# A sixteen-sequence layer kernel on one core: an own order of steps for each engine, the next sequence's front moved among the exponentials, maxima in halves, expert weights in eight pieces

## The chip, the cores and the metric

One core of a Trainium2 chip runs the whole program. Its engines are PE (TensorE, matrix products), ACT (ScalarE), DVE (VectorE), POOL (GpSimd) and SP (SyncE, which here only issues DMAs); each works through its own list of instructions, and they meet at semaphores. The metric is the device time of one execution in microseconds. The kernel before takes 1146.2 us, the median of three runs (1144.76 to 1148.17).

## The reference

Sixteen sequences of 256 tokens with 256 features pass four residual layers:

```python
x = x + x @ weight[subject].T + bias[subject]               # L0: one of 8 weights for each sequence
x = x + zX*lap_x(x) + zY*lap_y(x) + zR*x*(1 - x)            # L1: neighbours in both directions
# L2: 16 heads of 16 columns; q and own key, value from the side input, keys and values from x
q = (side + b_self) @ Wq + bq; k = (x + b_prev) @ Wk + bk; v = x @ Wv + bv
score_prev = q @ k.T / 4, masked beyond seq_len; score_self = (q * k_self).sum(-1) / 4
x = x + softmax([score_prev, score_self]) @ [v, v_self] @ Wo + bo
# L3: two shared dense layers s0, s1 and one of three chosen by the label (eo): relu(x @ wi) @ wo, F = 1024
w = softmax(relu([eo[0], s0[0], s1[0]] @ g1) @ g2)
x = x + eo * w[0] + s0 * w[1] + s1 * w[2]
```

All of it is float32. The kernel splits operands into a high and a low part and adds three products (hi·hi, lo·hi, hi·lo) for each.

## The kernel before, in words

Tiles are 128 partitions by 512 columns: both halves of the features side by side. A sequence goes through three groups of steps. The **front** makes x1, q, ks, lap, vs, kp, vp (x after L0, query, own key, the neighbours of L1, own value, key, value) and "self", the own scores. q and k are cut in three 16-bit parts each and copied by SP's DMAs (`place`, L386, six for each) into q_rows and k_rows, where one head's scores are a single product. The **attention** runs S0 to S15 (scores of a head, of which DVE takes the row maximum, L930), mT (transposes of the maxima, L591, cut in three parts by DVE, L941 to L944, and placed as three rows of q_rows by three DMAs, L421), and E0 to E15 (scores less maximum, transposed; ACT takes exponentials, L777, into prob, and the high part; the low part is DVE's for odd heads, L951, POOL's for even ones, L1136). The value products of head h (`attend`, L539, L540) follow E(h+3). DVE sums and normalises them in two halves ("half", "norm", "att", L961 to L974), PE transposes the result (aT, L516), multiplies by Wo ("wo"), and DVE makes x3T (L997). The **experts** are 12 hidden steps H (L488 to L490 into hid) and 12 output steps P (into out): after each H ACT makes the high part with relu (L821), DVE the low part (L1004), and the P two or so steps later reads both. Gates follow, then "mix", "scale", "sum" and "store".

The front's products, S, mT and E share two banks of PSUM in turns: a step waits (`open_bank`) until the one two places before it has been read. One bank of `pv` is used by the value products, by "self" and by aT.

The order of work is one list, BODY, built from FRONT and STEP (what is put behind each step of the front and attention). All engines go through it, each doing its part of a step; DVE has six steps of it put later (DVE_LATER). LAG says for which sequence a step of turn i is: front and S0 to S5 for sequence i, the rest of the attention and the first experts for i-1, the remaining experts for i-2. There are 18 turns: two written out, 14 in a hardware loop (FIRST = 2 to LAST = 16), two written out. In a turn come S6 to S15, mT, E0 to E15, then x1, q, ks, lap, vs, kp, vp, S0 to S5.

The chosen expert's weights are loaded as two DMAs of 1 MB into one buffer, raw; ACT makes high parts (L794) and POOL low parts (L1086), wi in one piece, wo in four. The two shared experts' weights are split once, in eight pieces (SHARED_AT, L787 and L1080), in turns 0 and 1.

## Time and profile before

| | |
|---|---|
| median of three runs | 1146.2 us |
| the profiled execution | 1148.4 us, its span 1146.8 us |
| one turn of the loop | 66.6 us, fourteen of them |
| busy in the span | PE 86%, DVE 76%, ACT 53%, POOL 50% |
| mean granted TensorE clock | 0.967 |
| DMA | 83.5 MB, 32% of the 16 queues' time |

The profile is one execution. An engine's busy time counts the union of its instructions; PE's matmuls overlap, so that each is drawn longer than the distance to the next. "Idle before" names the instruction whose completion ended an idle stretch. PE's granted clock is 1.00 at 2.4 GHz and 0.50 at 1.2 GHz.

### The profile page before, as it was taken

The page shows a single profiled execution, that of the slowest core. Times are in us where ns is not written, and L with a number is a line of the kernel's source. Part 1 is how long each engine was busy: PE and PEld are TensorE (multiplying, and loading weights), DVE is VectorE, ACT ScalarE, POOL GpSimd, SP SyncE. Part 2 cuts the span into 40 slices and gives each one's busy share as a digit, 9 for nine tenths or more (in the row PEclk, how much of TensorE's full clock was granted, in tenths as well). Part 3 has the DMA queues.
Part 4 walks back from the last instruction along what each step waited for, and adds up shares of the span by engine and source line. Part 5 has one row for each costly group of instructions (what it writes and reads, how often), then busy time and mean ns, then how long its engine had stood idle before and what let it go on. Part 6 is the DMA issues. An engine that isn't in the chain of part 4 may idle for free.

```text
span 1146.8 us, 27267 instructions
## 1 busy us (share of the span) xinstructions
PE 988.7 (86%) x9456; PEld 922.6 (80%) x9456; DVE 868.9 (76%) x1710; ACT 603.8 (53%) x1177; POOL 568.5 (50%) x432
## 2 busy tenths in 40 slices
PE   4558988998898999889899888989898898989886
PEld 4228888888888888888888888888888888888785
DVE  3576787877778787777878777787877778787733
ACT  3354654646565464656546455655645565554532
POOL 6573636455463645446364544636454463644422
PEclk9559999999999999999999999999999999999988
DMA  4725233251524324152422415242241524223110
GB/s 133 161 74 84 76 70 65 69 92 37 92 74 72 74 61 88 37 92 74 76 80 55 83 37 92 74 80 86 48 80 37 92 74 83 83 55 73 39 46 10
DMA packets 79339, 83.46 MB, mean 73 GB/s; under 512 B 11444, under 2 KB 74708, under 8 KB 79316
## 3 DMA queue, kind: packets, MB, share of 16 engines
q1 hardware_dynamic: 79316, 83.15, 32.0%
q8 instruction: 14, 0.23, 0.1%
q14 instruction: 9, 0.07, 0.0%
HBM read 53.37 MB, written 4.20 MB: 50 GB/s over the span
## 4 chain that ended last, share of the span: by engine, by line
PE 38%; DVE 30%; issue 12%; DMA 10%; ACT 6%; SPq 2%; POOL 1%; DVEq 1%; ACTq 0%; POOLq 0%
DMA k_rows<-prob_lo 7%; PE front L586 4%; DVE prob_hi L950 4%; PE out L488 4%; PE out L489 4%; PE out L490 4%; PE hid L488 4%; PE hid L490 4%; PE hid L489 4%; PE front L597 3%; DVE s_max L930 3%; DMA q_rows<-max_rows 3%; DVE hid_lo L1004 2%; PE front L488 2%; SPq L421 2%
## 5 line engine op out<-in xcount | busy, mean ns | idle before, releaser
L821 ACT ACTIVATE hid_hi<-hid 128x512 fp32r<-128x512 f32 x192 | 114.6, 597 | 251.5 <-PE hid L490 250.8
L488 PE MATMUL out<-hid_hi,exp_hi 128*128 128x256 f32 x768 | 230.1, 300 | 14.7 <-DVE hid_lo L1004 14.6
L1136 POOL TENSOR_TENSOR prob_lo<-prob,prob_hi 128x512 f16<-128x512 f32 x128 | 162.9, 1273 | 137.3 <-ACT prob_hi L781 137.3
L488 PE MATMUL hid<-x_hi,exp_hi 128*128 128x256 f32 x768 | 226.7, 295 | 2.2 <-DVE x_lo L1000 2.2
L930 DVE TENSOR_REDUCE s_max<-front 128x2 f32<-128x512 f32 x256 | 165.2, 688 | 77.0 <-PE front L586 76.0
L489 PE MATMUL out<-hid_lo,exp_hi 128*128 128x256 f32 x768 | 216.8, 282 | 0.0
L490 PE MATMUL out<-hid_hi,exp_lo 128*128 128x256 f32 x768 | 216.5, 282 | 0.0
L489 PE MATMUL hid<-x_lo,exp_hi 128*128 128x256 f32 x768 | 214.5, 279 | 0.0
L490 PE MATMUL hid<-x_hi,exp_lo 128*128 128x256 f32 x768 | 214.4, 279 | 0.0
L1086 POOL TENSOR_TENSOR exp_lo<-raw,exp_hi 128x512 fp32r<-128x512 f32 (+1 forms) x80 | 154.8, 1946 | 104.5 <-ACT exp_hi L794 104.3
L777 ACT ACTIVATE prob<-front 128x512 f32<-128x512 f32 x256 | 146.8, 600 | 63.4 <-PE front L597 61.7
L1004 DVE SCALAR_TENSOR_TENSOR hid_lo<-hid,hid_hi 128x512 fp32r<-128x512 f32 x192 | 131.0, 682 | 48.8 <-ACT hid_hi L821 48.8
L488 PEld LDWEIGHTS out<-hid_hi,exp_hi 128*128 128x128 f32 x768 | 146.1, 190 | 19.5 <-DVE hid_lo L1004 18.2
L488 PEld LDWEIGHTS hid<-x_hi,exp_hi 128*128 128x128 f32 x768 | 145.5, 189 | 3.3 <-DVE x_lo L1000 2.5
L489 PEld LDWEIGHTS out<-hid_lo,exp_hi 128*128 128x128 f32 x768 | 146.5, 191 | 0.0
L490 PEld LDWEIGHTS out<-hid_hi,exp_lo 128*128 128x128 f32 x768 | 146.3, 190 | 0.0
L489 PEld LDWEIGHTS hid<-x_lo,exp_hi 128*128 128x128 f32 x768 | 145.7, 190 | 0.0
L490 PEld LDWEIGHTS hid<-x_hi,exp_lo 128*128 128x128 f32 x768 | 145.0, 189 | 0.0
L950 DVE CAST prob_hi<-prob 128x512 f16<-128x512 f32 x128 | 86.2, 674 | 55.0 <-ACT prob L777 51.4
L597 PE MATMUL front<-q_rows,k_rows 100*128 100x256 bf16 x512 | 100.0, 283 | 27.3 <-DMA q_rows<-max_rows 18.5
L539 PE MATMUL pv<-v_cols,prob_hi 128*128 128x49 bf16 x1024 | 89.6, 187 | 32.2 <-DVE prob_lo L951 19.4
L539 PEld LDWEIGHTS pv<-v_cols,prob_hi 128*128 128x128 f16 x1024 | 72.4, 97 | 50.2 <-DVE prob_lo L951 25.2
(153 smaller groups left out, 2280.7 us busy)
## 6 DMA issues: line engine op xcount, KB each, us to landing
raw<-in_wi SPq DMA_DIRECT2D x16, 1024.0 KB, 4.9
raw<-in_wo SPq DMA_DIRECT2D x16, 1024.0 KB, 5.5
q_rows<-prob_hi SPq DMA_DIRECT2D x96, 128.0 KB, 4.2
k_rows<-prob_lo SPq DMA_DIRECT2D x96, 128.0 KB, 4.6
x_raw<-in_x SPq DMA_DIRECT2D x17, 256.0 KB, 2.7
w_raw<-in_w SPq DMA_DIRECT2D x17, 256.0 KB, 2.8
s_raw<-in_side SPq DMA_DIRECT2D x17, 256.0 KB, 3.5
out<-e_out SPq DMA_DIRECT2D x16, 256.0 KB, 2.2
```

The lines of the kernel that those rows point to most:

```text
L488: nc.tensor.matmul(acc, w_hi, a_hi, start=first, stop=False)
L489: nc.tensor.matmul(acc, w_hi, a_lo, start=False, stop=False)
L490: return nc.tensor.matmul(acc, w_lo, a_hi, start=False, stop=last)
L539: nc.tensor.matmul(acc, prob_hi[:, h % NPROB, at:at + P], v_cols[:, k, h, :], start=(k == 0), stop=False)
L597: last = nc.tensor.matmul(psum[:, k * S:(k + 1) * S], k_rows[0:ROWS_EXP, h, k * P:(k + 1) * P], q_rows[0:ROWS_EXP, h, :], start=True, stop ...
L777: last = nc.scalar.activation(prob[:, h % NPROB, :], psum[:, :], ACT.Exp, scale=SCALE)
L821: nc.scalar.activation(hid_hi[:, s % 2, :], hid_bank[s % 2][:, :], ACT.Relu).then_inc(hid_hi_done, 1)
L930: nc.vector.tensor_reduce(s_max[:, :, h:h + 1], psum, AX_X, ALU.max).then_inc(freed_dve, 1)
L950: linkf(nc.vector.tensor_copy(prob_hi[:, h % NPROB, :], prob[:, h % NPROB, :]))
L1004: nc.vector.scalar_tensor_tensor(hid_lo[:, s % 2, :], hid_bank[s % 2][:, :], 0.0, hid_hi[:, s % 2, :].bitcast(F32), ALU.max, ALU.subtract) ...
L1086: nc.gpsimd.tensor_tensor(exp_lo[:, CHOSEN, first:last], raw[:, at:at + last - first], exp_hi[:, CHOSEN, first:last].bitcast(F32), ALU.sub ...
L1136: nc.gpsimd.tensor_tensor(prob_lo[:, h % NPROB, :], prob[:, h % NPROB, :], prob_hi[:, h % NPROB, :], ALU.subtract).then_inc(prob_split_poo ...
```

## The change

BODY is replaced by five hand-written lists. In a turn the attention of sequence i-1 now starts at S0 (S0 to S11, then S12 to S15 among E0 to E4), the front of sequence i is spread between E7 and E12 (x1, q, lap, kp) and behind the last exponential (ks, vs, vp, self), and all experts are those of sequence i-2 (`lag`). Each kind of step has its own pair of semaphores, filled and freed.

- q_parts and k_parts get buffers of their own in what x_raw, w0_raw and x1T held, and SP places all rows behind E15 (its step "E15" waits for that product), the next inputs being loaded in "load" after the rows have landed.
- The maxima go in halves, m0 behind S9 and m1 behind H8: DVE cuts the three parts of eight heads on 128 partitions (scalar_tensor_tensor on 16 numbers each), PE transposes them as bf16 (two for each half), ACT copies them to max_rows, SP writes them in one DMA.
- Value products follow E(h+2). ACT makes the high part of all heads but 11, 13, 15 (before: the even ones), POOL the low part of 0, 2, 4, 6, 8, 9, 10, 12, 14.
- "norm" of the first eight heads goes to POOL, x2b to ACT; ACT makes a copy x3_kept of x3T, which "scale" reads.
- wi and wo are loaded and split in four pieces each.
- PE ends its turn with "logits_free", a wait for DVE's reading of the logits; "self" uses a front bank.

The core of the diff:

```diff
 
-EARLY = ["x1", "q", "ks", "lap", "vs"]
-ATTENTION = (["kp", "vp"] + [f"S{h}" for h in range(H)] + ["mT"] + [f"E{h}" for h in range(H)])
-USES = EARLY + ATTENTION
-USE = {name: n for n, name in enumerate(USES)}
-NU = len(USES)
-assert NU % 2 == 0
-
...
-STEP = [("S7", "H4 x_parts"), ("S8", "w_parts"), ("S9", "P3"), ("S10", "s_parts"), ("S11", "H5 wo_part0"),
-        ("S13", "P4 wo_part1"), ("S15", "H6 wo_part2"), ("mT", "P5 H7 P6 gate0 wo_part3"), ("E1", "H8"),
-        ("E2", "P7"), ("E4", "H9"), ("E6", "P8"), ("E10", "half H10"), ("E12", "norm P9 gate1"), ("E14", "H11"),
-        ("E15", "P10 pvend att"), ("x1", "P11 gate2 x1_parts"), ("q", "aT gate relu react"), ("ks", "logits"),
-        ("lap", "mix x2_parts scale wo"), ("vs", "x3_parts"), ("vp", "sum H0 self H1 P0 H2"), ("S1", "P1 wi_part"),
-        ("S3", "H3 store wo_load"), ("S5", "P2")]
-FIRST_HALF = ATTENTION.index("S5") + 1
...
+PE_BODY = """
+H0 S0 S1 H1 S2 S3 P0 S4 S5 H2 S6 S7 P1 H3 S8 S9 P2 m0 H4 S10 S11 P3 H5
+E0 S12 E1 P4 E2 S13 H6 E3 S14 P5 E4 S15 H7 E5 P6 E6 H8 m1 E7
+x1 P7 q E8 H9 E9 lap P8 E10 E11 H10 E12 kp P9 E13 H11 E14 P10 E15 P11 pvend
+ks aT vs gate wo logits vp self logits_free
+""".split()
+ACT_BODY = """
+H0 wi0 x3_keep H1 wi1 H2 wi2 wi3 H3 wo0 m0 H4 wo1 x_parts P3 H5 w_parts E0 E1 wo2 E2 H6 E3 wo3 E4 H7 E5 s_parts E6 H8 m1 E7
+x1_parts react q E8 P7 H9 E9 qa E10 x2_parts E11 qb H10 E12 kp E13 kq H11 E14 E15 P11
+ks aT vs x3_parts vp logits sum
+""".split()
+DVE_BODY = """
+S0 S1 H0 S2 S3 H1 S4 S5 S6 S7 H2 S8 H3 S9 x_parts S10 H4 gate0 S11 S12 H5 E1 S13 H6 S14 E3 S15 H7 E5 H8 E7
+x1 x1_parts react H9 half lap gate1 x2_parts H10 E11 kp E13 k3 H11 E15
+att gate2 aT relu wo x3_parts vp logits self mix scale
+""".split()
+POOL_BODY = """
+wi0 wi1 wi2 wi3 wo0 x_parts wo1 w_parts E0 wo2 E2 wo3 E4 s_parts E6 m1 x1 E8 qa E9 norm E10 qb E12 E14 ks vp sum
+""".split()
+SP_BODY = """
+load wo0 wo1 wo2 wo3 m0 m1 wi_load E15 kp k3 sum
+""".split()
...
+PRESENT = "load x_parts w_parts s_parts x1 x1_parts react q qa qb lap x2_parts ks vs kp kq k3 vp self".split()
+PREVIOUS = S_OF + E_OF + "m0 m1 half norm pvend att aT wo x3_parts wi_load".split()
+
+
+def lag(name):
+
+    return 0 if name in PRESENT else 1 if name in PREVIOUS else 2
+
+
...
+RING = [x for x in PE_BODY if family(x)[0]]
...
-PARTS = 5
+PARTS = 2 * STEPS
...
+BEHIND = 2
+HI_DVE = (11, 13, 15)
...
+        q_parts = [w0_halves[0], w0_halves[1], x1_halves[0]]
+        k_parts = [x1_halves[1], x_halves[0], x_halves[1]]
...
+                for n in range(STEPS):
+                    sp.dma_start(raw[:, n * C * F // STEPS:(n + 1) * C * F // STEPS].rearrange("p (k f) -> p k f", k=C),
+                                 wi[bass.ds(kind, 1), :, n * F // STEPS:(n + 1) * F // STEPS].rearrange("o (k p) f -> p (o k) f", p=P)
+                                 ).then_inc(raw_in[n], 16)
...
+                if name == "load":
+                    if isinstance(i, int) and i == 0:
+                        return
+                    who = chooser(subject_sb, i, w0.shape[0])
+                    wait(sp, q_placed, 16 * 6, i - 1, 16 * 6)
+                    load_w0(who)
+                    wait(sp, k_placed, 16 * 6, i - 1, 16 * 6)
+                    load_x(i)
+                    load_s(i)
+                    load_small(i, who)
+                elif name == "E15":
+                    wait_filled(sp, i, name)
+                elif name == "kp":
                     sp.dma_start(k_rows[MASK_ROW:MASK_ROW + 1, :, :],
                                  mask_dram[bass.ds(i, 1), :].unsqueeze(1).to_broadcast([1, H, S])).then_inc(mask_placed, 16)
...
+                    wait(sp, q_split, 1, i, 1)
                     place(q_rows, Q_BANDS, q_parts, 0, q_placed)
...
                     place(q_rows, Q_BANDS, q_parts, 1, q_placed)
...
                     place(q_rows, Q_BANDS, q_parts, 2, q_placed)
...
+                    wait(sp, k_part_done, 2 * C, i, 2 * C)
                     place(k_rows, K_BANDS, k_parts, 0, k_placed)
...
                     place(k_rows, K_BANDS, k_parts, 1, k_placed)
...
+                elif name == "k3":
+                    wait(sp, k_split, 1, i, 1)
                     place(k_rows, K_BANDS, k_parts, 2, k_placed)
...
+                elif name in ("m0", "m1"):
+                    half = int(name[1])
+                    wait_freed(sp, i, name)
+                    sp.dma_start(q_rows[ROWS_MAX:ROWS_EXP, half * HALF:(half + 1) * HALF, :], max_rows[:, :]).then_inc(max_placed, 16)
+                elif name == "wi_load":
                     kind = chooser(label_sb, i, wi.shape[0])
                     wait(sp, w_split, PARTS, i, SHARED)
                     load_wi(kind)
...
+                elif name[0:2] == "wo":
+                    n = int(name[2])
                     kind = chooser(label_sb, i, wo.shape[0])
...
+                    wait(sp, w_split, PARTS, i, SHARED + n + 1)
+                    load_wo(kind, n)
...
+                u, turn = RING.index(name), i + lag(name)
+                while True:
+                    u -= 2
+                    if u < 0:
+                        u, turn = u + len(RING), turn - 1
+                    seq = turn - lag(RING[u])
+                    if not isinstance(seq, int) or 0 <= seq < B:
+                        wait_freed(pe, seq, RING[u])
+                        break
+                    if turn < 0:
+                        break
...
+                if h == HALF:
+                    wait(pe, pv_freed, 1, i, 1)
...
+                elif name in ("m0", "m1"):
+                    half = int(name[1])
+                    wait(pe, max_split, 2, i, half + 1)
                     for t in range(C):
...
+                        last = nc.tensor.transpose(psum[0:3 * HALF, :].bitcast(BF16)[:, t * P:(t + 1) * P],
+                                                   m_parts[:, t, half, :], ident_half[:, :])
                 elif name[0] == "E":
                     h = int(name[1:])
...
+                    if h % HALF == 0:
+                        wait(pe, max_placed, 16 * 2, i, 16 * (1 + h // HALF))
...
+                elif name == "logits_free":
+                    wait(pe, logits_read, 1, j, 1)
...
+                elif name == "qa":
+                    wait_freed(act, i, "q")
                     nc.scalar.activation(q_parts[0], q_full[:, :, :], ACT.Copy).then_inc(q_part_done, 1)
+                elif name == "qb":
+                    wait(act, q_rest_done, 1, i, 1)
+                    nc.scalar.activation(q_parts[1], q_rest[:, :, :], ACT.Copy).then_inc(q_part_done, 1)
...
+                    wait(act, x3_done, 1, i - 1, 1)
+                    for c in range(C):
+                        last = nc.scalar.activation(x2b[:, c, :], react[:, c, :], ACT.Identity, bias=vec[:, c, BO:BO + 1])
+                    last.then_inc(x2b_done, 1)
+                elif name in ("m0", "m1"):
+                    half = int(name[1])
+                    heads = slice(half * HALF, (half + 1) * HALF)
+                    wait_filled(act, i, name)
+                    wait(act, max_placed, 16 * 2, i, 16 * half)
+                    nc.scalar.activation(max_rows[:, :], front_psum(name)[0:3 * HALF, :].bitcast(BF16)[:, 0:S], ACT.Copy).then_inc(freed["m"], 1)
+                    wait(act, d_self_done, 2, i, half + 1)
+                    nc.scalar.activation(p_self[:, :, heads], d_self[:, :, heads], ACT.Exp, scale=SCALE).then_inc(p_self_done, 1)
...
-                    if h not in DVE_PARTS:
+                    if h not in HI_DVE:
                         if h >= NPROB:
                             wait(act, pv_done, H, i, h - NPROB + 1)
                         last = nc.scalar.activation(prob_hi[:, h % NPROB, :], psum[:, :], ACT.Exp, scale=SCALE)
-                    last.then_inc(freed_act, 1)
+                    last.then_inc(freed["E"], 1)
...
+                elif name == "x3_keep":
+                    wait(act, x3_done, 1, j, 1)
+                    wait(act, chosen_added, 1, j - 1, 1)
+                    nc.scalar.activation(x3_kept[:, :, :], x3T[:, :, :], ACT.Copy).then_inc(x3_copied, 1)
...
+                    if h % HALF == HALF - 1:
+                        half = h // HALF
+                        heads = slice(half * HALF, (half + 1) * HALF)
+                        own, top = s_self[:, :, heads], s_max[:, :, heads]
+                        first, second, third = (m_parts[:, :, half, n * HALF:(n + 1) * HALF] for n in range(3))
+                        wait_freed(dve, i, name)
+                        nc.vector.scalar_tensor_tensor(top, top, 1.0, own, ALU.mult, ALU.max).then_inc(max_done, 1)
+                        wait(dve, max_done, 2, i, half + 1)
+                        linkf(nc.vector.tensor_scalar(first, top, -1.0, None, ALU.mult))
+                        nc.vector.scalar_tensor_tensor(m_rest[:, :, :], top, -1.0, first, ALU.mult, ALU.subtract)
+                        linkf(nc.vector.scalar_tensor_tensor(second, top, -1.0, first, ALU.mult, ALU.subtract))
+                        nc.vector.scalar_tensor_tensor(third, m_rest[:, :, :], 1.0, second, ALU.mult, ALU.subtract).then_inc(max_split, 1)
+                        nc.vector.scalar_tensor_tensor(d_self[:, :, heads], own, 1.0, top, ALU.mult, ALU.subtract).then_inc(d_self_done, 1)
...
+                elif name == "half":
+                    wait(dve, pv_done, H, i, HALF)
+                    wait(dve, p_self_done, 2, i, 1)
+                    heads = slice(0, HALF)
                     for t in range(C):
...
+                        sums = pv[:, t, 0:HALF * VW].rearrange("p (h w) -> p h w", w=VW)
+                        nc.vector.tensor_reduce(att[:, t, 0:HALF * DH].rearrange("p (h d) -> p h d", d=DH),
                                                 sums[:, :, 0:3 * DH].rearrange("p h (g d) -> p h d g", g=3), AX_X, ALU.add)
...
+                    sums = pv[:, :, 0:HALF * VW].rearrange("p t (h w) -> p t h w", w=VW)
+                    nc.vector.tensor_tensor(den[:, :, heads], sums[:, :, :, 3 * DH], p_self[:, :, heads], ALU.add).then_inc(pv_freed, 1)
+                    wait(dve, pv_freed, 1, i, 1)
+                    nc.vector.reciprocal(den[:, :, heads], den[:, :, heads]).then_inc(den_done, 1)
+                elif name == "att":
+                    wait(dve, pv_done, H, i, H)
+                    wait(dve, p_self_done, 2, i, 2)
                     wait(dve, own_done, 1, i, 1)
...
+                    heads = slice(HALF, H)
+                    sums = pv[:, :, 0:HALF * VW].rearrange("p t (h w) -> p t h w", w=VW)
+                    linkf(nc.vector.tensor_tensor(den[:, :, heads], sums[:, :, :, 3 * DH], p_self[:, :, heads], ALU.add))
+                    nc.vector.reciprocal(den[:, :, heads], den[:, :, heads])
                     for t in range(C):
...
+                        by_head = att[:, t, HALF * DH:D].rearrange("p (h d) -> p h d", d=DH)
+                        linkf(nc.vector.tensor_reduce(by_head, sums[:, t, :, 0:3 * DH].rearrange("p h (g d) -> p h d g", g=3), AX_X, ALU.add))
+                    for t in range(C):
+                        own = v_self[:, t, HALF * DH:D]
+                        linkf(nc.vector.tensor_tensor(att[:, t, HALF * DH:D], att[:, t, HALF * DH:D], own, ALU.add))
+                    for t in range(C):
+                        by_head = att[:, t, HALF * DH:D].rearrange("p (h d) -> p h d", d=DH)
+                        last = nc.vector.tensor_tensor(by_head, by_head, den[:, t, heads].unsqueeze(2).to_broadcast([P, HALF, DH]), ALU.mult)
+                    last.then_inc(att_done, 1)
...
+                elif name == "norm":
+                    cols = slice(0, HALF * DH)
+                    wait(pool, den_done, 1, i, 1)
+                    wait(pool, own_done, 1, i, 1)
+                    nc.gpsimd.tensor_tensor(att[:, :, cols], att[:, :, cols], v_self[:, :, cols], ALU.add).then_inc(norm_link, 1)
+                    wait(pool, norm_link, 1, i, 1)
+                    for t in range(C):
+                        by_head = att[:, t, cols].rearrange("p (h d) -> p h d", d=DH)
+                        last = nc.gpsimd.tensor_tensor(by_head, by_head, den[:, t, 0:HALF].unsqueeze(2).to_broadcast([P, HALF, DH]),
+                                                       ALU.mult)
+                    last.then_inc(half_done, 1)
```

## Rows read from the trace of the kernel before

**Rows 1.** The page, its parts 1 and 2: PE, and its granted clock in 40 slices.

```profile
PE 988.7 (86%) x9456; PEld 922.6 (80%) x9456; DVE 868.9 (76%) x1710; ACT 603.8 (53%) x1177; POOL 568.5 (50%) x432
...
PEclk9559999999999999999999999999999999999988
```

**Rows 2.** Stretches: length; busy us (x) of PE, PEld, DVE, ACT, POOL; PEclk; DMA.

```profile
480.30:546.88 66.58, 60.18 (x593) 56.75 (x591) 53.37 (x108) 37.08 (x73) 33.78 (x27) 1.00 0.32 71
1064.70:1086.80 22.10, 19.83 (x258) 18.32 (x259) 17.26 (x32) 15.32 (x30) 9.95 (x8) 1.00 0.15 49
1086.80:1097.20 10.40, 6.50 (x36) 5.68 (x35) 7.45 (x22) 3.09 (x8) 0.00 (x0) 0.71 0.01 2
1097.20:1146.80 49.60, 38.15 (x296) 37.37 (x296) 14.99 (x26) 14.92 (x27) 14.78 (x9) 0.88 0.10 33
```

**Rows 3.** Waits of PE in the same turn: us, times, longest; two of nine.

```profile
PE pv L539 <- DVE prob_lo L951: 1.1, 1, 1.1
...
PE front L586 <- DMA k_rows<-prob_lo: 0.6, 1, 0.6
```

**Rows 4.** Timeline of PE: start us, us long, line, tiles, idle before and releaser.

```profile
131.56 0.61 PE L597 MATMUL front<-q_rows,k_rows 100*128 100x256 bf16 x4 [0.67 <-DMA q_rows<-max_rows]
...
509.20 0.28 PE L489 MATMUL hid<-x_lo,exp_hi 128*128 128x256 f32 x1
509.31 0.28 PE L490 MATMUL hid<-x_hi,exp_lo 128*128 128x256 f32 x1
...
541.54 0.39 PE L597 MATMUL front<-q_rows,k_rows 100*128 100x256 bf16 x2 [0.39 <-ACT prob_hi L781]
...
542.06 0.36 PE L488 MATMUL hid<-x_hi,exp_hi 128*128 128x256 f32 x1
```

**Rows 5.** Timeline of ACT in that turn.

```profile
509.63 0.60 ACT L821 ACTIVATE hid_hi<-hid 128x512 fp32r<-128x512 f32 x1 [3.44 <-PE hid L490]
...
518.88 0.62 ACT L719 ACTIVATE p_hi<-w_raw 128x512 fp32r<-128x512 f32 x1
...
531.56 0.60 ACT L777 ACTIVATE prob<-front 128x512 f32<-128x512 f32 x1 [1.65 <-PE front L597]
532.05 0.59 ACT L781 ACTIVATE prob_hi<-front 128x512 f16<-128x512 f32 x1
...
540.88 0.60 ACT L781 ACTIVATE prob_hi<-front 128x512 f16<-128x512 f32 x1
```

**Rows 6.** Timeline of DVE in that turn.

```profile
482.80 1.22 DVE L950 CAST prob_hi<-prob 128x512 f16<-128x512 f32 x1 [0.21 <-DVE gate_terms L1019]
...
485.26 0.42 DVE L950 CAST prob_hi<-prob 128x512 f16<-128x512 f32 x1
...
486.89 0.56 DVE L961 TENSOR_REDUCE att<-pv 128x128 f32<-128x384 f32 x1 [0.48 <-PE pv L540]
...
488.71 0.49 DVE L974 TENSOR_TENSOR att<-att,den 128x128 f32<-128x128 f32 x2
...
503.47 0.42 DVE L922 TENSOR_TENSOR beside<-front,v_cols 128x256 f32<-128x256 f32 x1
...
504.80 1.02 DVE L926 TENSOR_SCALAR x2b<-react,vec 128x256 f32<-128x256 f32 x2
```

**Rows 7.** POOL's groups of instructions in that turn: busy us, mean ns, idle before.

```profile
L1136 POOL TENSOR_TENSOR prob_lo<-prob,prob_hi 128x512 f16<-128x512 f32 x9 | 11.5, 1274 | 10.7 <-ACT prob_hi L781 10.7
...
L1126 POOL TENSOR_TENSOR v_cols<-beside,v_cols 128x256 bf16<-128x256 f32 x2 | 1.4, 712 | 6.9 <-DVE v_cols L923 6.9
...
L1108 POOL TENSOR_TENSOR prob<-q_full,prob_hi 128x512 f32<-128x512 f32 x1 | 1.2, 1171 | 1.4 <-ACT prob_hi L743 1.4
```

**Rows 8.** SP's issues of k's rows: timeline, and median us to landing.

```profile
501.54 3.79 SPq L386 DMA_DIRECT2D k_rows<-prob_lo  x6
...
k_rows<-prob_lo SPq DMA_DIRECT2D x6, 128.0 KB, 4.4
```

**Rows 9.** POOL's splits of shared weights in the head, 45 to 67 us.

```profile
L1080 POOL TENSOR_TENSOR exp_lo<-raw,exp_hi 128x1024 fp32r<-128x1024 f32 x6 | 14.0, 2343 | 10.0 <-ACT exp_hi L787 10.0
```

395 lines of the change are left out of this document (162 added, 233 removed).

## The prediction

> **What bounds the kernel now.** I read five views in this order. The page first: TensorE (PE) is busy for 86% of the span at full granted clock, all but head and tail [rows 1]. It is the engine to follow, and what is left to win is its idle time. The table of stretches then gives one turn of the loop, 66.58 us, with PE busy 60.18 us of it in 593 matmuls [rows 2]. A turn after the first two repeats this within 0.1 us. The list of waits for the same turn has nine rows for PE, the longest 1.1 us, 6.2 us in all [rows 3]: no single wait is large. The timeline gives the pitch: a product follows the one before by 0.12 us but is drawn 0.28 us long [rows 4]. So each of the ten stalls hides another 0.16 us: idle is 6.2 + 1.6 + the 0.2 us of gaps too small to be listed = 8.0 us a turn, and the matmuls back to back need 58.6 us. No arrangement of this work gets a turn under that. The last view is the timelines of ACT, DVE, POOL and SP, for the durations below.
>
> Units: a hidden step H or an output step P is 12 products, 12 x 0.12 = 1.44, taken as 1.48 us with the change of operands, as are the front's six products at 1.42. An exponential's scores E with the eight value products behind it take 0.43 (bounded above by 541.54 to 542.06 [rows 4]).
>
> **Part by part.** I place one new turn against PE's own order, with E0 starting at 0, and see at each wait who is late.
>
> *Removed.* Nearly all of the 8.0 us of old stalls goes: rows of k before S0 (0.6 [rows 3]), maxima, their rows before E0, x2's parts, H2's bank, the last value products. Each was a chain with nothing queued in front; the new order puts 4 to 5 us of products there. The maxima in halves need one transfer each: m0 to E0 has H4, S10, S11, P3, H5 = 4.9 us for a chain that I estimate at 3.6 (two more operations of 0.4, an issue of 0.6 and a landing, which is bounded by 4.4 [rows 8]). PE's work grows by 0.1 us (four small transposes for two).
>
> *E0, S12, E1 (new).* E1 uses E0's bank, and ACT frees it only after both exponentials. ACT's order there is H5, w_parts, E0, and H5 is the step PE has just finished. ACT begins 0.32 us after the last matmul's start (509.31 to 509.63 [rows 4, 5]), so H5 at 0.20; 0.49 for it (pitch 531.56 to 532.05), 0.52 for w_parts (0.62 long), exponential from 1.21, second from 1.70, 0.60 long, done 2.30. PE follows such a release by 0.06 (540.88 + 0.60 to 541.54). E1 starts at 2.36; PE had only E0 and S12 to do, 0.41. Stall 1.95 us; at least 1.1 even with ACT free.
>
> *m1, x1.* x1 takes m1's bank. ACT is on H8 when m1 arrives: 0.45 us.
>
> *Exponentials 8 to 12.* Here the front meets three queues. ACT does q, E8, the kept output of P7, H9, in this order, so H9's high part ends at 22.8 and DVE's low part at 23.5. Behind it on DVE wait "half" (two reductions and a sum, 1.1 us) and then "lap" (0.75). PE's value products of head 8 wait for the former (0.5 us), E11 for the latter, which has its bank (0.85). On POOL q's remainder stands before E9's low part: it starts when ACT has done qa (24.4), takes 1.17, then 1.27 for E9 [rows 7]: head 9's products wait until 26.9, 0.9 us. POOL then does "norm", moved there from DVE, three operations, 1.8 us (between 1.2 and 2.1, by 0.71 for 256 elements), ahead of E10's low part: head 10's products wait another 1.0 (0.5 to 1.3). Together 3.25 us. The kernel before has 0.7 + 0.4 us here.
>
> *Last value products.* E15 is freed by one exponential, DVE splits it in 1.1 us, PE has P11 meanwhile: 0.25 us instead of 1.1.
>
> *att.* Now the transposes aT come behind ks alone (1.42 us). DVE needs for one half 486.89 to 489.20 = 2.3 us [rows 6]; the new sequence waits for itself between its reductions and sums, so 2.8, plus 0.2 to begin and 0.1 to release. Stall 1.7 (1.2 to 2.0). Before, x1, P11 and q covered it. Then wo waits 0.2 for the parts of aT.
>
> *logits_free.* PE ends the turn by waiting until DVE has read the logits, which DVE does behind vp: ACT's high part (0.25 + 0.65), DVE's four operations (503.47 to 504.80, 1.35 [rows 6]), two on the logits 0.45, release 0.1 = 2.8 us behind vp's end. PE has "self", 0.8. Stall 2.0 us; bounds 1.5 and 2.5. Queued behind it is H0, and so everything of the next turn.
>
> *S0 to H5.* DVE still has mix and scale, ACT the scaling of "sum" before H0's high part: P0 waits 0.35. The five small operations for m0 stand before H2's low part, in part while POOL works on weights: P2 waits 0.3 (0 to 0.9).
>
> *Rows behind E15.* SP issues thirteen transfers there, the first when E15's scores are done. Six take 3.8 us to issue, and one lands 4.4 us after issue [rows 8]: 8.3 + 4.4 = 12.7 us. PE's path from there to S0 is P11, the end of the turn, H0: 11.4 us of work and 4.2 of the stalls above. They are in time, with about 3 us to spare. The weights' eight pieces cost ACT 0.5 us more and POOL 0.4, hidden; SP's issues for them stand before m0 and wait for POOL, which is done by then.
>
> Casts: one took 1.22 us with a POOL operation under way, another 0.42 with none [rows 6]. Five of eight leave DVE. The Trainium skill, "SBUF — State Buffer", section "Who interferes with whom", says that such a cast and a GpSimd operation exclude each other for a whole instruction. By it up to 4 us of DVE's time comes free each turn; as DVE isn't what PE waits for, except at the points above, the sum stays.
>
> **Sum.** Stalls: 1.95 + 0.45 + 3.25 + 0.25 + 1.7 + 0.2 + 2.0 + 0.35 + 0.3 = 10.45 us in place of 8.0. Turn: 58.6 + 0.1 + 10.45 = 69.15 us.
>
> Ends: E0 of sequence 1 starts at 131.56 now [rows 4]. The new turn 1 has no experts, which saves some 7 us, but six of eight shared weight pieces move from before E0 into its exponentials, each 2.34 us on POOL [rows 9] and a load that waits for an earlier one: I take them as equal, 131.5 (bounds 124 and 137). Then 14 turns, 968.1. Tail from E0 of the last: now 22.1 + 10.4 + 49.6 = 82.1 [rows 2]. The experts of sequence 14 have 14 steps left there instead of 9, 7.4 us more; E1's wait and m1's transfer (nothing before it) add 3.8: 93.3. Span 131.5 + 968.1 + 93.3 = 1192.9. The profiled execution of before took 1148.4 for a span of 1146.8, and the median is 1146.2, 0.6 below the span: forecast **1192 us**, slower by 4%. Equality would need a turn of 65.9 us.
>
> **Rivals.**
> *B, the new stalls are half as large: faster.* Everything after E1 rests on PE arriving early. If products with changed operands take nearer 1.6 us, PE reaches head 8 to 10 later and the 3.25 us shrink to 1; and if DVE's waits for itself in att and its queue ahead of the logits cost half of what I took, another 2 go. Turn 69.15 - 2.25 - 2.0 = 64.9, total 131.5 + 909 + 93 = 1133. For it: PE's own step is the largest number here, and I took it at its lowest. Against: E1, att and logits_free are chains with next to nothing in front, whatever PE's pace. It decides at a turn of 65.9.
> *C, rows late.* Six transfers land after 4.4 us each [rows 8]; thirteen in a row may be bound by the engines that move them, not by their issue. If the last lands 5 us later than I count, the spare of 3 is gone and S0 waits 2 us a turn: 1192 + 28 = 1220.
> *D, the clock.* The granted clock was 0.71 in the stretch in which PE was busy for 6.50 of 10.40 us, and 1.00 in the whole turn [rows 2]. The new stretch from E15 to H0 has 8 of 12 us busy, in stalls of 1.7 and 2.0. If it falls to 1.2 GHz for some 4.6 us of work in each turn: 14 x 4.6 = 64, 1256. Beside it stands the Trainium skill, "TensorE: Matmul & The Clock Gate", section "HAM oscillation — how this bites in real kernels": waits that recur can throttle the array each time. The loop before, with waits up to 1.1 us, shows none of it.
> *E, no difference.* Partial forms of A and B cancel near 1146.
>
> **Chances.** A 0.62, B 0.24, C 0.06, D 0.04, E 0.04. A measurement of this kernel tells 0.3% (3.4 us) from no change. Faster 0.24, same 0.04, slower 0.72. The range reaches down over B, 1128, and up over most of C, 1216; A alone spans 1170 to 1212 (a turn of 67.6 to 70.4).
>
> **What would show it.** E1's row on PE with about 1.9 us before it, released by ACT; waits for "half", E11's bank, and POOL's low parts of 9 and 10, 3 us a turn; aT waiting 1.7 for DVE; the first product of H0 waiting 2 us for the read of the logits; none for k_rows. The turn's length between two x1 rows is the test: 69 right, under 66 B. I'm wrong if two of the four large stalls are missing.

## The result

| | before | after |
|---|---|---|
| median (lowest to highest), same chip | 1147.2 us (1144.8 to 1149.0), four runs | 1252.7 us (1248.9 to 1254.7), four runs |
| ratio, 95% interval | | 1.092 (1.088 to 1.095) |
| span of the profiled execution | 1146.8 us | 1252.9 us |
| mean granted TensorE clock | 0.967 | 0.932 |
| E0 of sequence 1 starts at | 131.56 us | 132.43 us |
| one turn of the loop | 66.6 us | 73.4 us (74.3 and 72.5 in alternation) |
| from the last E0 to the end | 82.1 us | 93.1 us |

The change makes the kernel 9% slower. The forecast was 1192 us, 4% slower, with a range up to 1216: right in sign, 61 us too low. Three terms make up the time, and two were met: the head (131.5 forecast, 132.4 measured) and the tail (93.3 and 93.1). All of the miss is in the turn, 73.4 us against 69.15: fourteen times 4.25 us are 59.5 us. The profile of after has to say where these 4.25 us are.

The page, PE's busy time and the clock in 40 slices, as [rows 1]:

```profile
PE 1046.6 (84%) x9488; PEld 966.4 (77%) x9488; DVE 834.9 (67%) x1615; ACT 682.6 (54%) x1401; POOL 619.8 (49%) x544
...
PEclk9668989999899998999999998999989999899988
```

PE is busy for 58 us more than before, with 32 more instructions among 9456, small transposes. Busy time grew and the work hardly did, and the row of the clock has 8s all through the loop, where before has 9s alone.

The table of stretches, as [rows 2]: two turns, then 2 us pieces at the end of the first, then the tail.

```profile
590.07:664.35 74.28, 65.24 (x594) 60.76 (x593) 51.39 (x100) 42.02 (x87) 37.05 (x33) 0.93 0.33 64
664.35:736.87 72.52, 62.62 (x594) 58.43 (x593) 51.95 (x101) 42.08 (x87) 37.13 (x33) 0.98 0.34 66
...
622.00:624.00 2.00, 1.08 (x11) 0.98 (x9) 1.52 (x4) 1.45 (x4) 0.00 (x0) 1.00 1.17 119
624.00:626.00 2.00, 0.63 (x3) 0.66 (x4) 1.69 (x9) 0.32 (x2) 1.29 (x2) 0.66 0.86 85
626.00:628.00 2.00, 2.00 (x11) 1.98 (x10) 0.63 (x1) 1.22 (x2) 0.71 (x1) 0.50 0.00 0
628.00:630.00 2.00, 2.00 (x11) 1.75 (x10) 1.24 (x3) 1.64 (x3) 1.92 (x3) 0.50 0.00 0
630.00:632.00 2.00, 2.00 (x14) 1.88 (x13) 0.71 (x3) 0.30 (x1) 1.17 (x1) 0.63 0.39 131
...
1159.84:1252.90 93.06, 73.27 (x660) 69.44 (x658) 40.48 (x83) 40.20 (x80) 31.23 (x27) 0.89 0.10 29
```

The granted clock is 0.50, the lower level, for more than 6 us behind a stretch in which PE is half idle. The turn of before stands at 1.00.

PE's waits in the two turns together, as [rows 3], by what ended them: us in total, times, longest.

```profile
PE hid L520 <- DVE gate_s L1090: 4.6, 2, 2.3
PE front L623 <- DVE s_max L986: 3.9, 2, 1.9
PE pv L578 <- POOL prob_lo L1206: 3.3, 4, 1.0
PE out L520 <- DVE hid_lo L1066: 2.6, 2, 1.3
PE pv L548 <- DVE att L1036: 2.4, 2, 1.2
PE front L636 <- DVE react L955: 0.8, 2, 0.4
PE front L520 <- ACT max_rows L823: 0.6, 2, 0.3
```

The timeline of PE, as [rows 4]: the end of the wait in front of head 9's value products and the fall behind it, the end of the turn, then E0, S12 and E1.

```profile
599.84 0.20 PE L578 MATMUL pv<-v_cols,prob_hi 128*128 128x49 bf16 x1 [1.04 <-POOL prob_lo L1206]
...
600.61 0.28 PE L521 MATMUL hid<-x_lo,exp_hi 128*128 128x256 f32 x1
600.73 0.37 PE L522 MATMUL hid<-x_hi,exp_lo 128*128 128x256 f32 x1
...
601.54 0.41 PE L520 MATMUL hid<-x_hi,exp_hi 128*128 128x256 f32 x1
601.75 0.41 PE L521 MATMUL hid<-x_lo,exp_hi 128*128 128x256 f32 x1
...
622.12 0.96 PE L614 MATMUL front<-head_ones,ksT 128*128 128x16 f32 x8
...
625.37 0.55 PE L520 MATMUL hid<-x_hi,exp_hi 128*128 128x256 f32 x1 [2.29 <-DVE gate_s L1090]
625.72 0.41 PE L521 MATMUL hid<-x_lo,exp_hi 128*128 128x256 f32 x1
625.94 0.41 PE L522 MATMUL hid<-x_hi,exp_lo 128*128 128x256 f32 x1
...
631.50 0.61 PE L623 MATMUL front<-k_rows,q_rows 97*128 97x256 bf16 x4
...
647.13 0.39 PE L636 MATMUL front<-q_rows,k_rows 100*128 100x256 bf16 x2
...
649.45 0.39 PE L623 MATMUL front<-k_rows,q_rows 97*128 97x256 bf16 x2 [1.93 <-DVE s_max L986]
```

Behind 625.37 the pitch of products is 0.21 us and each is drawn 0.41 us long, where [rows 4] have 0.11 to 0.12 and 0.28. From there to 631.50 PE does H0, S0, S1 and H1, which at the pitch of 2.4 GHz take 3.3 us. The pattern repeats in pairs of turns: in one the clock is low for 3.4 us near head 9 (here from 600.8) and for 6.8 at the end of the turn, in the other for 3.4 us at the end of the turn alone. What that costs can be read from the distance of each of PE's instructions to the next, set against the median distance of the same pair at 1.00: in the low stretches of the first turn they lie 4.2 us further apart, in those of the second 1.6, 2.9 us a turn in the mean. (A stretch of 3.4 us at half the clock can't lose more than 1.7.) So the turns alternate between 74.3 and 72.5.

DVE at the chain in front of m0, and what POOL does meanwhile, as [rows 6] and [rows 7]:

```profile
637.01 0.97 DVE L993 SCALAR_TENSOR_TENSOR s_max<-s_max,s_self 128x16 f32<-128x16 f32 x1
638.01 1.20 DVE L995 TENSOR_SCALAR m_parts<-s_max 128x16 bf16<-128x16 f32 x1
639.24 0.18 DVE L996 SCALAR_TENSOR_TENSOR m_rest<-s_max,m_parts 128x16 f32<-128x16 f32 x1
...
639.72 0.69 DVE L1066 SCALAR_TENSOR_TENSOR hid_lo<-hid,hid_hi 128x512 fp32r<-128x512 f32 x1
```

```profile
636.64 2.54 POOL L1149 TENSOR_TENSOR exp_lo<-raw,exp_hi 128x512 fp32r<-128x512 f32 x2 [2.46 <-ACT exp_hi L848]
```

Two operations on 16 elements a partition last until POOL's two splits of weights end, at 639.2; the third, with POOL idle, takes 0.18 us. The six small operations together delay H2's low part by 2.7 us, and P2 waits for it.

The page on the transfers behind E15, as [rows 8], KB each and us to landing:

```profile
q_rows<-w_raw SPq DMA_DIRECT2D x80, 128.0 KB, 4.3
k_rows<-x1T SPq DMA_DIRECT2D x48, 128.0 KB, 6.6
k_rows<-x_raw SPq DMA_DIRECT2D x48, 128.0 KB, 7.9
```

The last rows of k land 7.9 us after their issue, not 4.4. SP's last issue ends at 619.6, so they land at 625 to 627, and S0 starts at 628.08: the 3 us to spare of the forecast are nearly nothing.

### The profile page after: what moved, and what is told of

Same layout as the page of the kernel before. It is cut to its first block, busy times and chain, and to the rows that moved or that the text cites. A ratio compares the mean times of both kernels' runs of the same rounds, so it can differ in the third digit from the quotient of the medians.

```text
span 1252.9 us, 27580 instructions
## 1 busy us (share of the span) xinstructions
PE 1046.6 (84%) x9488; PEld 966.4 (77%) x9488; DVE 834.9 (67%) x1615; ACT 682.6 (54%) x1401; POOL 619.8 (49%) x544
## 4 chain that ended last, share of the span: by engine, by line
POOL 30%; issue 29%; PE 23%; DVE 12%; ACT 3%; DMA 1%; POOLq 1%; SPq 0%; ACTq 0%; DVEq 0%
POOL exp_lo L1149 11%; POOL prob_lo L1206 10%; PE out L520 3%; PE out L521 2%; PE out L522 2%; PE front L520 2%; DVE gate_terms L1081 2%; PE hid L520 2%; POOL e_out L1178 1%; PE hid L521 1%; PE hid L522 1%; PE front L522 1%; POOL s_lo L1159 1%; PE front L521 1%; PE pv L578 1%
## 5 line engine op out<-in xcount | busy, mean ns | idle before, releaser
L520 PE MATMUL hid<-x_hi,exp_hi 128*128 128x256 f32 x768 | 244.1, 318 | 33.9 <-DVE gate_s L1090 33.9
L1206 POOL TENSOR_TENSOR prob_lo<-prob,prob_hi 128x512 f16<-128x512 f32 x144 | 173.2, 1203 | 118.6 <-ACT prob_hi L836 118.1
L522 PE MATMUL hid<-x_hi,exp_lo 128*128 128x256 f32 x768 | 230.0, 300 | 0.0
L521 PE MATMUL hid<-x_lo,exp_hi 128*128 128x256 f32 x768 | 230.0, 300 | 0.0
L1149 POOL TENSOR_TENSOR exp_lo<-raw,exp_hi 128x512 fp32r<-128x512 f32 x128 | 167.5, 1314 | 115.3 <-ACT exp_hi L848 115.1
L1066 DVE SCALAR_TENSOR_TENSOR hid_lo<-hid,hid_hi 128x512 fp32r<-128x512 f32 x192 | 131.5, 685 | 125.6 <-ACT hid_hi L872 125.6
L520 PEld LDWEIGHTS hid<-x_hi,exp_hi 128*128 128x128 f32 x768 | 158.8, 207 | 38.0 <-issue 33.0
L521 PEld LDWEIGHTS hid<-x_lo,exp_hi 128*128 128x128 f32 x768 | 159.9, 208 | 0.0
L522 PEld LDWEIGHTS hid<-x_hi,exp_lo 128*128 128x128 f32 x768 | 159.0, 207 | 0.0
L623 PE MATMUL front<-k_rows,q_rows 97*128 97x256 bf16 x512 | 93.8, 299 | 38.4 <-DVE s_max L986 28.9
L836 ACT ACTIVATE prob_hi<-front 128x512 f16<-128x512 f32 x208 | 124.7, 600 | 0.0
```

The source lines that it names most:

```text
L520: nc.tensor.matmul(acc, w_hi, a_hi, start=first, stop=False)
L521: nc.tensor.matmul(acc, w_hi, a_lo, start=False, stop=False)
L522: return nc.tensor.matmul(acc, w_lo, a_hi, start=False, stop=last)
L623: last = nc.tensor.matmul(psum[:, t * S:(t + 1) * S], q_rows[0:ROWS_MAX, h, t * P:(t + 1) * P], k_rows[0:ROWS_MAX, h, :], start=True, stop ...
L836: last = nc.scalar.activation(prob_hi[:, h % NPROB, :], psum[:, :], ACT.Exp, scale=SCALE)
L1066: nc.vector.scalar_tensor_tensor(hid_lo[:, s % 2, :], hid_bank[s % 2][:, :], 0.0, hid_hi[:, s % 2, :].bitcast(F32), ALU.max, ALU.subtract) ...
```

## Theories

Theory A, the clock: the low stretches are the largest part of the miss (2.9 of 4.25 us; some expectations say 3.6, from a coarser reading), and each follows from long waits of PE. Theory B, the waits themselves: some are longer than forecast, and a lower clock costs little, since a later wait takes it up. Theory C, the rows: they are what would bound the turn once a wait in front of them is gone. The first runs alter one order each; the later ones separate the clock from the waits. Where an expectation below names its theories by other letters, its own words hold.

## Experiments on the single orders

**The logits read ahead of the values.** DVE at the end of the turn:

```diff
-att gate2 aT relu wo x3_parts vp logits self mix scale
+att gate2 aT relu wo x3_parts logits vp self mix scale
```

> DVE reads the gate's logits ahead of vp instead of behind it; nothing else changes. In the changed kernel PE waits 2.29 us for that read at the end of every turn, and the granted clock is 1.2 GHz for some 6 us after it. Theory A (the wait costs itself and also lowers the clock, which costs another 2.8 us): the wait goes, no low clock behind it, a turn falls from 73.4 to 68.3 us, the whole from 1253 to 1180. Theory B (the low clock lies where PE would wait anyway and costs nothing): only the wait goes, a turn of 71.1, 1220. Theory C (something else is late at the same place, x3's parts or the rows of k): a turn above 72.5, over 1238.

Measured: 1251.5 us (1246.2 to 1259.5), ratio 1.093 (1.087 to 1.098): no gain that can be told. PE's waits in two turns:

```profile
PE front L623 <- DMA k_rows<-x_raw: 4.3, 2, 2.2
...
PE hid L520 <- issue: 0.8, 2, 0.4
```

The wait of 2.3 us for the logits became one of 0.4, and a new wait of 2.2 us for the rows of k stands three steps on. The two waits lay over each other, as Theory C has it.

The length of the turns says more than the total. Two turns of the same profiled execution:

```profile
438.03:509.59 71.56, 61.38 (x594) 57.07 (x593) 52.18 (x101) 41.82 (x87) 37.06 (x33) 1.00 0.34 66
800.86:875.93 75.07, 65.66 (x594) 60.83 (x593) 51.77 (x100) 41.76 (x87) 37.07 (x33) 0.93 0.33 63
```

In seven turns in a row (151.7 to 652.7 us) the clock stays at 1.00 and a turn takes 71.6 us; in the last five it falls three times, for 3.4 us each, and a turn takes 75.1. The program is the same and the long waits are the same (2.2 us for k's rows, 1.9 in front of S12, 1.2 for att), so 3.5 us of these turns are the clock's. It also shows that waits of 2.2 and 1.9 us in each turn need not bring the clock down.

**P4 between E0 and S12.** PE's order:

```diff
-E0 S12 E1 P4 E2 S13
+E0 P4 S12 E1 E2 S13
```

> PE does the output step P4 before S12 instead of behind E1. Both things that hold PE there are covered by it: S11's maximum, which stands behind gate0 on DVE (1.93 us seen), and E0's release by ACT, which does H5 and w_parts first (2.28 us after E0 seen, as forecast). Theory: the 1.93 us go, a turn falls by 1.9 to 71.5, the whole to 1226. Rival: P4 waits for the kept output of the first expert at that place, or E2's value products come late, and the turn keeps more than half of it: over 72.5, 1240.

Measured: 1237.6 us, ratio 1.080 (1.077 to 1.082), turn 72.0 in most turns and 72.3 in the mean. The 1.9 us in front of S12 became 0.6, and 0.6 came in front of E2; the low clock near head 9 comes in five of thirteen turns, in place of every second, and the one behind the logits remained in all but one. The wait that was forecast at 1.95 us is real, and filling it is worth 1.1 to 1.4 us.

**H2 ahead of S7's maximum and its chain.** DVE's order:

```diff
-S5 S6 S7 H2 S8 H3
+S5 S6 H2 S7 S8 H3
```

> DVE makes H2's low part before S7's maximum and the five small operations for m0, instead of behind them (these took 2.7 us, 637.01 to 639.72, two of them 0.97 and 1.20 long with POOL at work). Theory: P2's wait of 1.3 us goes (1.8 us between the starts), a turn falls by 1.5 to 1.8 us, the whole to 1229. Rival: S9 or m0 now waits for the delayed maximum of S7 instead: less than 0.7 us a turn, over 1243.

Measured: 1229.5 us, ratio 1.072 (1.068 to 1.075), turn 71.7 over three turns (71.0 to 72.7 but for the loop's first). P2's wait is gone from the list. The step forecast at 0.3 us is worth 1.6 us a turn.

**Head 9 ahead of q's remainder on POOL:**

```diff
-s_parts E6 m1 x1 E8 qa E9 norm E10 qb E12 E14
+s_parts E6 m1 x1 E8 E9 qa E10 norm qb E12 E14
```

> POOL makes E9's low part before q's remainder and E10's before norm. In the changed kernel PE waits 1.04 us for the one and 0.17 or 1.03 us for the other, and in every second turn the granted clock falls behind these waits too (600 to 604 us). Theory (the queue on POOL, as forecast): both waits fall under 0.3 us, the second low stretch goes, a turn is 71.6 us, the whole 1228. Rival: the value products of head 8 and E11, which wait for DVE, then take the same time: a turn above 72.7, over 1243.

Measured: 1227.3 us, ratio 1.071 (1.070 to 1.073), turn 71.7. The waits for POOL's prob_lo are gone; kp now waits 1.0 us for x_lo, as before had it. Near head 9 the clock stays high; one stretch of 3.4 us a turn is left, behind the logits in some turns and behind the 1.9 us in front of S12 in others.

**All four together.** The four diffs above.

> The four orders of the other runs together: logits ahead of vp, P4 ahead of S12, H2's low part ahead of S7's maximum, POOL's low parts first. Seen alone: P4 1.4 us a turn, H2 1.6, logits 1.1 but with a wait of 2.2 us for the rows of k in its place. Theory C (the rows, placed behind E15, are the bound behind the wait for the logits): PE waits 2 to 4 us for k_rows in each turn, a turn is about 67.5 us, the whole 1170, still slower than the kernel before. Theory without C: no such wait, under 65.5, faster than the kernel before.

Measured: 1179.1 us, ratio 1.029 (1.027 to 1.031), turn 68.3, granted clock 1.00 in eleven of thirteen turns. PE waits 2.2 us a turn for k's rows; in two turns a low stretch of 3.4 us follows that wait, and these take 69.8 and 69.7 us.

**Rows of q and k by halves of heads, and the logits first.** The first half of each of the twelve transfers goes out after E7, the second behind E15 (q's and k's columns are sorted by halves, so that each transfer stays one piece):

```diff
-load wo0 wo1 wo2 wo3 m0 m1 wi_load E15 kp k3 sum
+load wo0 wo1 wo2 wo3 m0 m1 wi_load E7 qb kp k3 E15 vs sum
...
-    sp.dma_start(rows[band * DH:(band + 1) * DH, :, :], parts[n]).then_inc(done, 16)
+    sp.dma_start(rows[band * DH:(band + 1) * DH, half * HALF:(half + 1) * HALF, :], parts[n][:, half, :]).then_inc(done[half], 16)
```

> Logits ahead of vp, and the rows of q and k placed by halves of heads: heads 0 to 7 as soon as E7 is done and the parts are there, heads 8 to 15 behind E15, 24 transfers of 64 KB instead of 12 of 128 KB, the columns of q and k sorted so that a half is one half of the features. Theory C (rows late): the wait of 2.2 us for k_rows at S0 goes, and S8 waits for nothing: a turn of 69.2 us, the whole 1192. If the logits' wait and the rows were not what holds the turn's end: no change against e1_logits, 1250. If 26 transfers cost more than they give (SP's issue before m0, S8 late): over 1215.

Measured: 1225.4 us, ratio 1.069 (1.067 to 1.071), turn 71.7. The wait for the rows is gone, and the clock is low for 3.4 us in every turn, behind the 1.9 us in front of S12. Against the first run, which differs by the rows alone, it is 26 us, 1.9 a turn. That isn't the price of the late rows: where the first run has its clock at 1.00 its turn is 71.6 us too, and the 26 us lie mostly in its turns of 75.1. What the late rows cost at an equal clock these two runs don't show.

**The rows by halves and all four orders.**

> All four orders and the rows by halves. By the sum of what each gives alone: 73.4 - 2.3 (logits) - 1.8 (clock) - 1.4 (P4) - 1.6 (H2) - 1.5 (POOL) = 64.8 us a turn, 131 + 14 x 64.8 + 91 = 1129, faster than the kernel before by 1.5%. If the waits only hand on to one another: over 67, over 1160.

Measured: 1157.1 us, ratio 1.010 (1.008 to 1.012), turn 67.05, clock 1.00 in the loop. So five edits, none of which touches what is computed or where the front stands, take off 96 of the 105 us that the change had added. The single gains in the turn (1.7 with the rows, 1.1 to 1.4, 1.7, 1.7) sum to 6.2 to 6.5 us, and together they give 6.35. Each also holds what its edit did to the low clock, so that the match may be chance.

**The rows by halves alone,** a control.

> The changed kernel with one thing altered: the rows of q and k are placed by halves of heads (24 transfers in place of 12), the first half after E7, the second behind E15. No order of an engine and no wait of TensorE is moved. In the changed kernel TensorE waits 2.3 us for the end of the logits at this place, and with that wait gone 2.2 us for the rows, so the two waits lie over each other. Theory A (the clock): with the logits wait in its place the rows hide behind it, and the turn stays at 73.4 us, 1253 us in all (1247 to 1258), low clock in every turn as before. Theory B (the late rows are a cost of their own beside the logits): the turn falls by up to 1 us, to 1239. This is the control for the next kernel.

Measured: 1249.6 us, ratio 1.090 (1.087 to 1.092), turn 73.4, the same waits to 0.1 us. No cost of the rows can be told while the logits are late.

## Experiments on the clock

**Products nobody reads, ahead of the wait for the logits** (fillers):

```diff
 elif name == "logits_free":
+    for _ in range(16):
+        nc.tensor.matmul(hid_bank[0][:, 0:S], lin_hi[:, 0, 0:P], lin_hi[:, 1, 0:S], start=True, stop=True)
     wait(pe, logits_read, 1, j, 1)
```

> The changed kernel with sixteen matmuls of 256 columns (constants, into a bank that nobody reads at that time, 1.9 us at the high clock) in front of PE's wait for the logits: the wait's end stays where it is, but PE is busy until then. Theory A (the clock is a cost of its own): the granted clock stays 1.00 behind the wait, a turn falls by 2.8 us to 70.6, the whole to about 1212. Theory B (the low clock is hidden): no change, 1250 to 1256; if the fillers delay the turn, slower.

Measured: 1235.7 us, ratio 1.080 (1.076 to 1.083), turn 71.6. PE has 1.9 us more to do in each turn, and the kernel is 17 us faster. In the profiled execution (1231.7 us, the fastest of the four, mean clock 0.961) no low clock is left in twelve of thirteen turns, not even near head 9; the slowest, 1239.5 us, has a mean clock of 0.950. DVE's read of the logits is no earlier, so this gain is the clock's.

**Fillers at both long waits, rows by halves.** To the rows by halves, the fillers above and 14 behind E0:

```diff
-E0 S12 E1 P4 E2
+E0 warm S12 E1 P4 E2
...
+elif name == "warm":
+    wait(pe, hid_split, LSTEPS, j, 5)
+    for _ in range(14):
+        nc.tensor.matmul(hid_bank[0][:, 0:S], lin_hi[:, 0, 0:P], lin_hi[:, 1, 0:S], start=True, stop=True)
```

> The kernel with rows by halves, plus TensorE products whose result nobody reads: 14 of 128x256 in front of the wait for the maximum of S12 and 16 in front of the wait for the logits. 14 x 0.12 = 1.7 us and 16 x 0.12 = 1.9 us, each shorter than the wait behind it (1.9 and 2.3 us), so no product that counts starts later or earlier by them. The output is the reference's. Theory A (the low clock after long waits is the largest part of the miss, 3.6 us of a turn: 5.6 us of work at half speed behind the logits cost 2.8 us, 3.2 us behind E9 and E10 in every second turn cost 0.8): turn 69.8 us, 1203 us in all (1195 to 1213), granted clock 1.00 in the loop or low only behind E9 in every second turn. Theory B (the clock costs little, since later waits take it up again): turn above 72.5 us, 1240 or more.

Measured: 1225.3 us, ratio 1.069 (1.066 to 1.071), turn 71.65. Between the two expectations: 1.75 us a turn came back, not 3.6. The stretches:

```profile
585.00:587.00 2.00, 2.00 (x17) 1.98 (x13) 1.11 (x1) 0.10 (x1) 1.92 (x4) 0.67 0.00 0
587.00:589.00 2.00, 1.82 (x15) 1.27 (x14) 1.06 (x2) 1.62 (x3) 1.97 (x2) 0.50 0.00 0
...
611.00:613.00 2.00, 2.00 (x20) 1.92 (x19) 1.33 (x3) 2.00 (x4) 0.77 (x1) 1.00 0.00 0
```

H0 runs at 1.00 now (the last row). Near heads 8 and 9 the clock still falls, behind a wait of 1.03 us for head 9's prob_lo from POOL, and now in every turn.

**Fillers there too:** nine products between E10's product and the value products of head 8.

```diff
 last.then_inc(filled[family(name)[0]], 1)
+if name == "E10":
+    for _ in range(9):
+        nc.tensor.matmul(hid_bank[0][:, 0:S], lin_hi[:, 0, 0:P], lin_hi[:, 1, 0:S], start=True, stop=True)
```

> The kernel with rows by halves and filled waits, plus 9 TensorE products nobody reads (1.1 us) between E10's product and the value products of head 8, whose prob_lo comes 1.0 us late from GpSimd (the gap in the products is 1.42 us). That was the only place left with the low clock: 3.5 us of every turn at 1.2 GHz. Theory A (the low clock is worth what is left to explain): no low clock anywhere in the loop, turn 71.65 - 1.4 = 70.2 us (69.9 to 70.8), 1205 us in all (1200 to 1214). Theory B (later waits take it up again, as they did in the kernel before with its added wait, where 3.5 us of low clock cost 0.6 us): turn 71.0 to 71.6, 1217 to 1225.

Measured: 1220.7 us (1220.5 to 1221.2), ratio 1.065 (1.063 to 1.067), turn 71.2. This one went to its Theory B. The late prob_lo is head 9's, and not head 8's as the expectation has it: the nine products fill the short waits ahead of it. The clock is 1.00 in the whole loop, and the turn fell by 0.45 us only. PE's gaps near heads 9 and 10 say why, first without these nine products, then with them:

```profile
584.74 0.20 PE L589 MATMUL pv<-v_cols,prob_hi 128*128 128x49 bf16 x1 [1.03 <-POOL prob_lo L1223]
...
587.91 0.22 PE L589 MATMUL pv<-v_cols,prob_hi 128*128 128x49 bf16 x1 [0.18 <-POOL prob_lo L1223]
```

```profile
582.56 0.20 PE L589 MATMUL pv<-v_cols,prob_hi 128*128 128x49 bf16 x1 [0.88 <-POOL prob_lo L1226]
...
585.72 0.20 PE L589 MATMUL pv<-v_cols,prob_hi 128*128 128x49 bf16 x1 [1.04 <-POOL prob_lo L1226]
```

With the clock low between them PE waits 0.18 us at head 10's products; with the clock held it waits 1.04. Both start 12.9 us after x1's sum, as POOL's chain takes as long in both. The low stretch and the stall for head 10 lay over each other, and only the last part of the stretch, behind head 10, cost anything.

**And H2 ahead of S7.** The diff shown above, on top.

> The kernel of the run above with H2's subtraction on the vector engine moved in front of S7's maximum and its chain of small operations, which ends the 1.3 us wait in front of P2 (the gap is 1.91 us; the forecast had 0.3 us for it). With the low clock gone and this step at its forecast, all the rest is as the forecast had it. Theory A (clock and P2 are the whole miss of the turn): turn 69.0 us (68.6 to 69.6), the forecast's 69.15, and 1190 us in all (1184 to 1200). Theory B (something else is left): turn above 69.8, 1202 or more.

Measured: 1198.0 us (1197.4 to 1198.1), ratio 1.045 (1.043 to 1.046). A turn, and the waits of two:

```profile
562.93:632.56 69.63, 65.43 (x633) 61.79 (x632) 51.41 (x100) 41.85 (x87) 37.08 (x33) 1.00 0.24 68
```

```profile
PE pv L589 <- POOL prob_lo L1226: 3.8, 4, 1.0
PE pv L559 <- DVE att L1056: 2.4, 2, 1.2
```

With the clock held and P2's wait gone, the turn is 69.6 us, between the two expectations (the first ended at 69.6, the other began at 69.8) and 0.5 above the forecast's 69.15. Against the 73.4 us of after, the clock and P2 account for 3.8.

**The other direction: a wait added to the kernel before.** If a wait is what lowers the clock, it must do so there. Three reductions that nobody reads, ahead of x2's low part on DVE:

```diff
 elif name == "x2_parts":
+    for n in range(3):
+        nc.vector.tensor_reduce(spare[:, 2 * n:2 * n + 2], lin_hi[:, n, :].bitcast(F32).rearrange("p (a b) -> p a b", a=2), AX_X, ALU.max)
     wait(dve, x2_hi, 1, i, 1)
```

> The kernel BEFORE, with three reductions of 128x512 on the vector engine whose result nobody reads, in front of the subtraction that makes x_lo of x2. By the 0.6 us of a maximum they delay x_lo by 1.8 us, and TensorE's wait for it in front of kp grows from 1.0 to 2.8 us. Nothing else is altered. Theory A (in this kernel's stream a wait of some 2 us or more is followed by a stretch at 1.2 GHz): the turn grows by the 1.8 us and by 1.6 to 3.6 us more, to 70.0 to 72.0 us, 1195 to 1222 in all, with granted clock 0.5 behind the wait. Theory B (the low clock of the changed kernel has another cause, such as its denser mix of small products): the turn grows by the wait alone, 68.4 us, 1171 us (1165 to 1178), clock 1.00 in the loop.

Measured: 1183.6 us (1180.7 to 1185.2), ratio 1.033 (1.030 to 1.035); turns of 68.8 to 69.8. The wait, and 2 us pieces around its end at 582.15:

```profile
PE front L489 <- DVE x_lo L874: 2.7, 1, 2.7
```

```profile
580.70:582.70 2.00, 0.55 (x5) 0.58 (x5) 1.97 (x4) 0.00 (x0) 0.00 (x0) 1.00 0.04 5
582.70:584.70 2.00, 2.00 (x15) 2.00 (x14) 1.23 (x2) 1.20 (x3) 0.00 (x0) 0.68 0.00 0
584.70:586.70 2.00, 2.00 (x11) 2.00 (x11) 1.82 (x5) 1.09 (x4) 0.00 (x0) 0.50 0.23 60
586.70:588.70 2.00, 2.00 (x19) 2.00 (x19) 1.38 (x6) 2.00 (x5) 0.00 (x0) 0.97 1.00 149
```

In a kernel whose loop had no low stretch the clock is low for 3.4 us, in five of six turns read, behind the wait that was put in and nowhere else. The sixth has the same wait, no low clock, and takes 68.7 us.

**The same with 20 fillers in the wait,** ahead of PE's wait for x_lo:

```diff
 elif name == "kp":
+    wait(pe, hid_split, LSTEPS, i - 2, 11)
+    for _ in range(20):
+        nc.tensor.matmul(hid_bank[0][:, 0:S], lin_hi[:, 0, 0:P], lin_hi[:, 1, 0:S], start=True, stop=True)
     wait(pe, x2_split, 1, i, 1)
```

> The kernel before with the three reductions of the run above and 20 TensorE products of 128x256 that nobody reads (2.4 us) in front of the wait for x_lo. Theory A: the wait is filled, the clock stays at 2.4 GHz, and only the 1.8 us of the delay are left: turn 68.4 us, 1171 us (1165 to 1178), so 20 to 50 us less than the run above although TensorE has more to do. Theory B (the clock has nothing to do with the wait): the same as the run above within 0.5%.

Measured: 1178.4 us (1176.6 to 1179.1), ratio 1.028 (1.026 to 1.030), turn 68.7, clock 1.00. The mechanism of Theory A holds in both runs. Its price doesn't: the two differ by 5 us (their intervals touch), 0.4 us a turn for a stretch in which PE's instructions lie 1.5 us further apart. With the clock held, PE waits 0.9 us at hid_lo and 0.8 for the rows of k; without, 0 and 0.3 to 0.7. Most of the lost time lay in front of waits that were there anyway.

## Experiments for a faster version

The variant of 67.05 us still had waits in front of S12, E2, kp, aT and H0. Three more kernels go on from it.

**gate0, w_parts, P4 and x2_parts:**

```diff
-E0 P4 S12 E1 E2                 (PE)
+E0 S12 P4 E1 E2
-S10 H4 gate0 S11 S12 H5 ... H7 E5 H8      (DVE)
+S10 H4 S11 S12 H5 ... H7 E5 gate0 H8
-lap gate1 x2_parts              (DVE)
+lap x2_parts gate1
-H5 w_parts E0 E1                (ACT)
+H5 E0 w_parts E1
-wo1 w_parts E0                  (POOL)
+wo1 E0 w_parts
```

> The fastest variant so far (rows by halves, logits ahead of the values, H2 ahead of S7, GpSimd's head 9 ahead of q's rest; turn 67.05 us), with P4 behind S12 in place of ahead of it, gate0 moved from ahead of S11 to behind E5 on the vector engine, w_parts behind E0 on the scalar engine and GpSimd, and x2_parts ahead of gate1. Expected to go: the waits in front of S12 and E2 (gaps 0.84 and 0.95 us, of which 0.3 stay) and in front of kp (gap 1.18, 0.2 stays): 67.05 - 2.4 = 64.7 us a turn (64.2 to 65.5), 1122 us in all (1114 to 1134), below the kernel before. If instead the vector engine has no free 1.3 us behind E5 (in the trace it idles 2.0 us there), H8's or E7's subtraction comes late and the turn stays above 66 us, 1140 or more.

Measured: 1152.6 us (1152.2 to 1152.9), ratio 1.005 (1.004 to 1.007), turn 66.8: a miss. The waits for S12, E2 and kp went as expected, but head 11's cast and subtraction stand behind gate1 on DVE, and PE waits 1.2 us for them.

**A new order of the end of the turn,** vs ahead of aT and vp ahead of gate:

```diff
-ks aT vs gate wo logits vp self logits_free      (PE)
+ks vs aT vp gate wo logits self logits_free
-ks aT vs x3_parts vp logits sum                  (ACT)
+ks vs aT vp x3_parts logits sum
-relu wo x3_parts logits vp self                  (DVE)
+relu wo logits x3_parts vp self
```

> The run above with the end of the turn in another order as well: vs ahead of aT and vp ahead of gate, so that the two 1.45 us products cover the norm of the heads and the split of its transpose (gap in front of aT 1.50 us), and the logits read ahead of x3_parts. The wait in front of aT goes; what follows wo is shorter (logits and self, 1.2 us, in place of 2.7), so H0 waits about 1.0 us for x3_lo. Net 0.5 to 1.0 us less than the run above: 64.0 us a turn (63.4 to 64.8), 1112 us in all (1103 to 1124). If the x3 chain is longer than 2.3 us, the gain is given back in front of H0 and the time is that of the run above.

Measured: 1161.9 us (1158.5 to 1164.9), ratio 1.014 (1.012 to 1.016), turn 67.1, the clock low for 3.4 us in four of six turns: another miss, and slower than the one above. The wait for att went (1.2 us), and H0 waits 1.7 us for x3_lo in its place, followed by the low clock in most turns; those without it are as long (67.0 to 67.2). The two products can cover the chain in front of wo or the one behind it.

**gate1 behind H11.** The diff of the last run but one, with

```diff
-lap x2_parts gate1 H10 E11 kp E13 k3 H11 E15
+lap x2_parts H10 E11 kp E13 k3 H11 gate1 E15
```

> The kernel of e15 with gate1 moved on the vector engine from behind x2_parts to behind H11. In e15 the x2 part is earlier, but gate1's two operations (1.5 us) stand ahead of head 11's cast and subtraction, and TensorE waits 1.2 us for that prob_lo (gap 1.64 us). Behind H11 the vector engine idles 1.56 us, which holds gate1. If that wait goes and nothing takes its place: turn 66.85 - 1.2 = 65.6 us (65.3 to 66.1), 1135 us in all (1129 to 1142), ratio 0.985 to 0.996, faster than both kernels. If the cast of head 11 is late anyway, since GpSimd's work at the same time makes the subtraction 1.5 us long in place of 0.7, the turn stays above 66.4 and the time above 1146.

Measured: 1138.0 us (1137.8 to 1138.1, five runs), before 1145.9 beside it, ratio **0.993 (0.992 to 0.994)**: faster than both kernels. A turn, and PE's longest waits in two:

```profile
600.28:666.10 65.82, 61.72 (x594) 57.23 (x593) 51.27 (x101) 41.54 (x87) 37.94 (x33) 1.00 0.25 72
```

```profile
PE pv L559 <- DVE att L1047: 2.5, 2, 1.2
PE front L647 <- DVE react L966: 0.8, 2, 0.4
```

The turn is 65.8 us, within the 65.3 to 66.1 expected. One wait above 0.4 us is left. The forecast had put equality with before at a turn of 65.9; here 65.8 gives 8 us less than before, as the time outside the fourteen turns is 215 us (1136.3 less 14 x 65.8), 10 less than in after.

## Why the forecast was right in sign and 61 us too low

By its own steps, gaps in PE's starts less the work in them, per turn:

| step | forecast | measured | |
|---|---|---|---|
| E0, S12, E1 | 1.95 | 2.1 | E0 at 647.13, next at 649.45 |
| m1, x1 | 0.45 | 0.35 | ACT max_rows |
| heads 8 to 12 | 3.25 | 2.9 | prob_lo, react, den |
| last value products | 0.25 | 0 | |
| att | 1.7 | 1.4 | DVE att |
| wo | 0.2 | 0.3 | |
| logits_free | 2.0 | 2.4 | 622.12 to 625.37, less self |
| P0 | 0.35 | 0 | |
| P2 | 0.3 | 1.5 | DVE hid_lo |
| sum | 10.45 | 10.95 | |
| low clock | 0 | 2.9 | |
| rest | | 0.85 | 73.4 - 58.7 - 10.95 - 2.9 |

*Removed, and the dense time.* The old stalls did go, and the work is the same. Right.

*E0, S12, E1.* The size is right, and the bank's chain is there to the hundredth: ACT's second exponential starts at 648.81 and is 0.60 long, 2.28 us behind E0 where 2.30 was worked out. That the gap stands in front of S12 wasn't seen: gate0 delays S11's maximum on DVE, to nearly the same moment. So the term was right with half of its reason; P4's move, which answers both, gave back 1.1 to 1.4 us.

*Heads 8 to 12, att, wo, logits_free.* The mechanisms, their releasers and within 0.5 us their sizes are as forecast. These are the four large stalls that had to be there.

*P2.* The term is mis-sized, 0.3 forecast and 1.5 measured, although its upper bound of 0.9 named the cause. The operations on 16 elements (five by the forecast, six in the trace) were priced by their number; what counts is that two of them fall beside POOL's splits and last until these end. Over the kernel the operation of L995 takes 0.17 us at least, 1.15 in the median and 2.27 at most. The Trainium skill, "SBUF — State Buffer", section "Who interferes with whom", counts such an operation with a scalar among those that can contend with GpSimd for a pair of ports, and then the later one waits for the whole instruction of the other. The trace agrees, with 1.20 beside POOL and 0.17 to 0.18 for its neighbours behind it.

*The clock.* This is the step that failed. It stood in the forecast as rival D, with its place (the end of the turn) and a price (4.6 us of work a turn at 1.2 GHz) that gives 1256, and with a chance of 0.04 and outside the range. That 1256 is close to the 1252.7 measured is luck: D had 64 us for the clock alone, and holding the clock gave back 2.2 us a turn, 31 in all; the rest of the 61 us is P2 and the gaps named below. The reason given against it was that waits up to 1.1 us in the loop before show no low clock. But the forecast itself had made waits of 2.0 and 1.95 us, with 1.7 us before the one, and the only row about such a stretch, the 0.71 of the tail [rows 2], spoke for the fall. The evidence was for a waiting pattern that the new kernel no longer had. The Trainium skill, "TensorE: Matmul & The Clock Gate", section "HAM oscillation — how this bites in real kernels", describes a loop in which the same wait for a transfer is followed by the low clock in every pass. The trace agrees for the 2.29 us wait, which is followed by it in every turn, and not for the waits near heads 8 and 9, where it comes in every second.

*Rows behind E15.* They arrive in time, but the 3 us to spare were nearly nothing: the transfers land 6.6 and 7.9 us after issue where one of before lands after 4.4 [rows 8]. Rival C was right about this size, and it cost nothing here only because the logits were later still. It shows as soon as they aren't.

*B and E* needed the stalls to be small. They weren't.

*Head and tail.* The tail was worked out, and met. The head wasn't: two effects of opposite sign were taken as equal, with bounds 13 us apart, so that its hit within 0.9 us is luck.

So by the table the miss of 4.25 us is 2.9 of clock, 0.5 of stalls (P2 1.2 too low, the others 0.7 too high in sum), and a rest of 0.85, in gaps too small to be read one by one, whose cause stays open. What the clock costs in the end is less than what it loses. From H0 to P0 the two turns of after take 6.50 and 5.30 us, and 3.91 with the clock held, 2.6 and 1.4 more; near head 9 the first turn loses 0.5. The mean of the two is 2.2 us, which is what holding the clock in all three places gave back (73.4 to 71.2).

What stays open: why the pattern near head 9 comes in every second turn in one kernel, in every turn in another and in none in a third, with the same waits ahead of it; why the 1.93 us in front of S12 are followed by low clock in every turn of the variant with the logits and rows, in some turns of the kernels with the logits, H2 or POOL's order alone, and not in the kernel after; why the kernel with the logits' order alone runs seven turns without low clock and then five with three stretches each; what the late rows cost at an equal clock; and what H2's gain would be without POOL's weights beside the chain. None of these was tried.

## To carry to other kernels

When a change makes new waits of about 2 us on TensorE in each turn of a loop, price the work behind them at 1.2 GHz as well, and let the range reach there, although such a wait doesn't always bring the clock down; waits of 1.1 us in the old loop say nothing about 2.3 in the new. Read the length of every turn and not of two: the clock can differ between turns of one execution. Before taking a wait away, list what is due next behind it: here the logits' read and the rows of k hid each other, and each of the two edits alone was worth nothing. A small operation is priced by what runs beside it on the other engine, not by its elements.

## What the runs showed of the hardware

- Waits of TensorE of 2.29 us (after, in every turn), 1.93 us (the variant with logits and rows, in every turn), 1.7 us (the new end of the turn, in four of six) and 2.7 us (added to before, in five of six) were followed by low clock for 3.4 or 6.8 us, and near heads 8 and 9 waits of 0.17, 0.41 and 1.04 us in a row were, in every second turn of after. The wait of 1.2 us for att was followed by none.
- The same waits were followed by no low clock elsewhere: 1.93 us in every turn of the kernel after; 2.2 and 1.9 us in seven turns of the kernel with the logits' order, whose last five turns have three stretches each (71.6 against 75.1 us); 2.2 us in eleven of thirteen turns with all four orders. So the length of a wait alone doesn't decide.
- What a low stretch of 3.4 us cost in the end ran from nothing (the new end of the turn) over 0.4 us (before with its added wait) to 1.4 (all four orders, 69.8 against 68.3).
- Unread products in the wait kept the clock at 2.4 GHz in twelve of thirteen turns: 16 of them, 1.9 us of TensorE work, made the kernel 17 us faster.
- Twelve transfers in a row from one place of the SBUF to another, 128 KB each, landed 4.3 us after their issue in the median for the first five, and 6.6 and 7.9 for k's behind them; six in a row had landed after 4.4 [rows 8].
- An operation on 16 elements took 0.17 us at the least and 1.20 beside a POOL operation, 2.27 at the most.
